# The first products of two expert layers, 36 and 136 columns wide in place of 256

## The reference

```python
# first expert layer: 8 experts, rank 16, the two best are taken
logits = x @ W_router.T                       # 8 columns
probs  = softmax(logits); combine = normalised weights of the two best
h      = einsum('nd,erd->ner', x, A)          # 8 * 16 = 128 columns
out    = x @ W_base.T + b_base + einsum('ner,eor->no', h * combine[:, :, None], B) * 2.0

# second expert layer: 4 experts, rank 8, the best one is taken
logits = x @ gate_w.T + expert_bias           # 4 columns
z      = einsum('nh,erh->ner', x, lora_A)     # 4 * 8 = 32 columns
out    = x @ W_up.T + (z of the best expert) @ lora_B
```

## Time and profile before

| | |
|---|---|
| median of 3 timed runs | 1790.31 us (1788.58 to 1790.43) |
| the profiled execution's own time | 1790.04 us |
| its span, first to last instruction | 1788.5 us |
| mean granted clock of TensorE | 0.974 |
| TensorE busy | 1688.1 us, 94% of the span |
| first expert layer, T(0) to the transposes of L697 | 154.8 to 189.3 us |
| second expert layer, block of the low parts to the end | 1723.5 to 1788.5 us |

### The profile page before, as it was taken

One profiled execution on the slowest core, in us unless ns is written; L12 is line 12 of the kernel. 1 busy time (PEld: TensorE's weight loads), 2 busy tenths in 40 slices (PEclk: granted clock), 3 DMA queues, 4 the chain that ended last, 5 costly groups with the idle time before them and its releaser, 6 DMA issues. The chain is left out here.

```text
span 1788.5 us, 26687 instructions
## 1 busy us (share of the span) xinstructions
PE 1688.1 (94%) x9420; PEld 1378.5 (77%) x9420; DVE 1199.0 (67%) x1847; ACT 1267.6 (71%) x2165; POOL 726.3 (41%) x786
## 2 busy tenths in 40 slices
PE   5998797999999999999999999999999999999839
PEld 4776575888888888888888888888888888888627
DVE  5565676766776677667766776677667766776853
ACT  3332146987798779877987798779877987798611
POOL 2543121444344434443444344434543454344620
PEclk9998898999999999999999999999999999999969
DMA  4220124333233323322333233323332323231121
GB/s 153 98 86 1 53 83 136 109 100 105 77 113 100 102 79 114 99 100 82 114 95 102 83 114 92 106 83 112 91 109 83 110 89 113 83 108 66 60 74 48
DMA packets 99429, 166.46 MB, mean 93 GB/s; under 512 B 11713, under 2 KB 49985, under 8 KB 97889
## 3 DMA queue, kind: packets, MB, share of 16 engines
q1 hardware_dynamic: 99296, 164.75, 28.8%
HBM read 158.43 MB, written 6.29 MB: 92 GB/s over the span
## 5 line engine op out<-in xcount | busy, mean ns | idle before, releaser
L217 PE MATMUL bank<-xh,w_h 128*128 128x512 f32 x1152 | 463.5, 402 | 9.6 <-DVE m_xc L1275 7.7
L218 PE MATMUL bank<-xl,w_h 128*128 128x512 f32 x1152 | 451.0, 392 | 0.0
L219 PE MATMUL bank<-xh,w_l 128*128 128x512 f32 x1152 | 450.1, 391 | 0.0
L1071 POOL TENSOR_TENSOR m_z_l<-m_zg,m_z_h 128x512 fp32r<-128x512 f32 x128 | 178.0, 1391 | 575.6 <-ACT m_z_h L1197 575.6
L1125 ACT ACTIVATE m_mt<-m_mt,m_unit 128x128 f32<-128x128 f32 x1024 | 312.1, 390 | 0.0
L1050 POOL TENSOR_TENSOR w_l<-w_raw,w_h 128x512 fp32r<-128x512 f32 x144 | 185.9, 1291 | 242.2 <-ACT w_h L1092 242.2
L1286 DVE TENSOR_TENSOR x<-x,bank 128x512 f32<-128x512 f32 x128 | 87.9, 687 | 273.7 <-PE bank L219 273.7
L217 PEld LDWEIGHTS bank<-xh,w_h 128*128 128x128 f32 x1152 | 217.4, 189 | 62.9 <-issue 19.7
L219 PEld LDWEIGHTS bank<-xh,w_l 128*128 128x128 f32 x1152 | 217.2, 189 | 46.5
L1275 DVE SCALAR_TENSOR_TENSOR m_xc<-bank,m_par_conv,m_xc 128x1020 f32<-128x1020 f32 (+2 forms) x192 | 244.6, 1274 | 12.0 <-ACT m_xc L1104 7.1
L218 PEld LDWEIGHTS bank<-xl,w_h 128*128 128x128 f32 x1152 | 217.6, 189 | 41.1
(11 more groups left out here) (238 smaller groups left out, 2771.6 us busy)
## 6 DMA issues: line engine op xcount, KB each, us to landing
m_mt<-ncs_rows SPq DMA_DIRECT2D x128, 512.0 KB, 3.8
w_raw<-w_in SPq DMA_DIRECT2D x144, 256.0 KB, 3.0
m_wo_raw<-w_out_in SPq DMA_DIRECT2D x64, 256.0 KB, 5.2
m_e<-ecs_rows SPq DMA_DIRECT2D x128, 128.0 KB, 3.5
a_wo_raw<-wo_in SPq DMA_DIRECT2D x8, 1024.0 KB, 4.9
x<-x_in SPq DMA_DIRECT2D x8, 256.0 KB, 4.6
a_wq_raw<-wq_in SPq DMA_DIRECT2D x8, 256.0 KB, 3.9
e_wb_raw<-f_base SPq DMA_DIRECT2D x2, 1024.0 KB, 7.8
```

Of the source, the lines that this page charges most:

```text
L217: nc.tensor.matmul(out, ah, bh, start=first, stop=False)
L218: nc.tensor.matmul(out, ah, bl, start=False, stop=False)
L219: return nc.tensor.matmul(out, al, bh, start=False, stop=last)
L1071: nc.gpsimd.tensor_tensor(z_l[:, s % 2, :, :], zg[:], f(z_h[:, s % 2, :, :]), ALU.subtract).then_inc(zl_ready, 1)
```

## The change

`a` becomes as wide as it needs to be: 136 columns in the first layer (544 numbers a row) and 36 in the second (144). The tile, its high and low part and the moving side of the 12 matmuls of each P(t) shrink with it. The zero fill, its semaphore and SyncE's wait for it are gone; with them goes `combine_block`'s whole program on GpSimd. Nothing is reordered.

```diff
-AW = 256
@@ attention_block, GpSimd @@
-                next_weights.pad(pool)
@@ ExpertWeights @@
-        self.a = [sb("wa_raw", [P, KT, AW]), sb("wa_h", [P, KT, AW], F32R), sb("wa_l", [P, KT, AW], F32R)]
+        width = self.ER + experts
+        self.a = [sb("wa_raw", [P, KT, width]), sb("wa_h", [P, KT, width], F32R), sb("wa_l", [P, KT, width], F32R)]
-        self.pad_zeroed = taken(nc, sems, f"{tag}_pad_zeroed")
-    def pad(self, pool):
-        self.nc.gpsimd.memset(self.a[0][:], 0.0).then_inc(self.pad_zeroed, 1)
-
     def load(self, sp):
...
-        sp.wait_ge(self.pad_zeroed, 1)
         sp.dma_start(raw[:, :, 0:ER], w_a).then_inc(self.loaded, 16)
@@ experts_block, products(t) @@
-                        last = three_pass(nc, bank[:, 2 + t % 2, 0:AW], xh[:, k, tok], xl[:, k, tok],
+                        last = three_pass(nc, bank[:, 2 + t % 2, 0:ER + experts], xh[:, k, tok], xl[:, k, tok],
                                           wa_h[:, k, :], wa_l[:, k, :], k == 0, k == KT - 1)
@@ combine_block @@
-            @block.gpsimd
-            def _(pool):
-                next_weights.pad(pool)
```

## The result

| | before | after |
|---|---|---|
| median of 10 timed runs each, side by side | 1790.45 us (1788.58 to 1792.23) | 1794.88 us (1793.9 to 1796.74) |
| profiled execution | 1790.04 us | 1794.77 us |
| its span | 1788.5 us | 1793.1 us |
| mean granted clock | 0.974 | 0.971 |
| first expert layer, T(0) to L697 (now L690) | 34.42 us | 35.07 us |

The ratio is 1.0027 (95% interval 1.0019 to 1.0036). The forecast was slower, 1796.4 us. The rows of the table from T(0) to the end of the second layer explain the profiled difference: T(0) starts at nearly the same time (1732.94 and 1732.87), and +0.74, +4.03, +1.52 and -1.56 follow, 4.7 us together.

What follows compares the result with a forecast made beforehand. GpSimd was taken to bound the second layer's entry, TensorE the rest. Entry -2.6, loads -0.7, clock +9.2 and first layer +0.2 made +6.1 on 1790.04 us, 1796.1; the timed median lies 0.3 above: 1796.4 us, range 1787.0 to 1801.0.

Steps and rivals of the forecast that it cites:

- zero fill and its wait: Two GpSimd fills of 0.95 us and SyncE's wait go; costed at 0, covered by the x loads.
- ScalarE's high part of A: Second layer's entry: 144 columns per row instead of 1024, 0.35 us instead of 1.06, -0.7 us.
- entry together, block to T(0): Second layer, block's start to first transposes: high part -0.7 and GpSimd's low part -1.9, together -2.6 us.
- a P product at full clock: Narrow products, both layers: the weight load bounds, 0.106 us each against 0.117 before.
- clock rises later, second layer: Second layer's start: thin first products delay steady streaming by 2.6 us, half of it lost, +1.3 us.
- T(3) to B(2): Second layer's narrow stretch: clock falls 4.5 us in, the rest takes twice as long, +5.9; narrower products -0.6 us.
- B(2) at half clock: Second layer: tile 2's wide base products start at half clock, half of 4.0 us lost, +2.0 us.
- first layer: Cheaper narrow products of tiles 1 to 4 -0.5, later clock rise +0.7, no fall of the clock: +0.2 us.
- the loads: Second layer: 72 narrow products at full clock, each now costing only its weight load, -0.7 us.
- The full-precision rate: Rival: narrow products run at the rate of full-precision matmuls, 0.23 us for 136 columns; 1795.4 to 1803 us, chance 0.11.
- the faster rival: Rival: narrow products shrink to their columns and VectorE decides, or clock holds and loads bound; 1782.4 to 1786.5 us, chance 0.10.
- That the clock holds: Rival: second layer's clock stays up or falls late in the narrow stretch; 1789.5 us, chance 0.22.

Runs made afterwards that it cites:

- e1_only: Kernel before with only the second layer's first products narrow (36 columns), zero fill and wait kept: 1795.48 us beside 1789.8, ratio 1.0028.
- e1_wide: Changed kernel, second layer's parts made on 36 columns but products 256 wide over zero fill: 1788.93 us beside 1789.8, ratio 0.9997.
- e1_136: Changed kernel, second layer's parts made on 36 columns but products 136 wide over zero fill: 1787.73 us beside 1789.44, ratio 0.9990.
- e0_only: Kernel before with only the first layer's first products narrow (136 columns): 1789.56 us beside 1789.8, ratio 1.0001.
- spread: Changed kernel, second layer's wide base products of tile 2 cut in four slices, one behind each of P(2) to P(5): 1787.2 us beside 1789.8, ratio 0.9991.
- dve_wide: Kernel before, with VectorE instead of GpSimd making the second layer's base low part: 1786.26 us beside 1789.44, ratio 0.9983.
- spread_wide: Kernel before, products 256 wide, second layer's base products of tile 2 in four slices behind P(2) to P(5): 1790.92 us beside 1789.44, ratio 1.0007.
- spread_dve: Changed kernel, second layer's base products of tile 2 spread among narrow products, and base low part on VectorE: 1785.21 us beside 1789.44, ratio 0.9976.
- w136_dve: Changed kernel, second layer's parts on 36 columns, products 136 wide over zeros, base low part on VectorE: 1783.84 us beside 1789.93, ratio 0.9970.

## Why the prediction held

The forecast's sign and its cause, a fall of the clock in the second layer that B(2) inherits, are shown: 36 columns lose it, 136 and 256 keep it with the rest of the kernel alike, and wide products between narrow ones keep it in the profile and, by their mean clock, in nine of eleven executions. By its own steps, in us of the profiled executions:

| step | predicted | measured | by |
|---|---|---|---|
| zero fill and its wait | 0 | not to be seen | weights requested 3.69 and 3.68 us behind x; `e1_only` keeps both and is as slow |
| ScalarE's high part of A | -0.7 | -0.74 for itself | 1.06 to 0.32 |
| entry together, block to T(0) | -2.6 with the high part | -1.13, without it | 9.48 to 8.35 |
| a P product at full clock | 0.106 | 0.11 | starts in both layers |
| clock rises later, second layer | +1.3 | T(0) to T(3) +0.74 | 13.27 to 14.01 |
| T(3) to B(2) | +5.9 - 0.6 | +4.03 | 10.98 to 15.01 |
| B(2) at half clock | +2.0 | +1.52 | 5.60 to 7.12 |
| first layer | +0.2 | T(0) to L697 +0.65 | 34.42 to 35.07 |
| last part | 0 | -1.56 | 25.69 to 24.13 |

**The total was in part luck.** The sum had +6.1 us; the profiles show +4.7 and the medians +4.4. It had +8.5 from T(0) to L697 of the second layer (9.2 for the clock, less 0.7 for the loads), where 6.3 were measured, and nothing for the last part, which gave 1.6 back. Against this, it had T(0) 2.4 us earlier, and it came 0.07 earlier. Two errors of over 2 us took each other away.

**The entry was mis-sized.** GpSimd's three parts did end 1.85 us sooner after the block's start, as predicted. That L142 would still meet them was wrong: L164, reached during the part of `b`, is held through both remaining parts, and 0.72 of the gain goes to the steps behind it. The prediction had this case among its bounds ("if L166 were itself held until the last part, 0.5 us would be given back (-1.4)"); the measured -1.1 lies 0.3 beyond that bound. In the profile the entry's whole gain then vanished in the later landing of the weights (T(0) only 0.07 us earlier). The lower ratios of `e1_wide` and `e1_136` agree with a gain that is there when the clock holds; their intervals reach 1.0006 and 0.9999, so each by itself shows little, and `e1_136` was also spared the second fall of the clock (below), which is worth as much.

**The moment of the fall was right, its price too high.** Predicted 4.5 us behind T(3), measured 4.6 (5.3 in `e1_only`). The 4.5 had been set above both rows it came from (2.5 and 3.8), so that it was met this closely is luck too. And the first of these rows was read wrongly: the 3.8 us behind the last wide matmul were not idle to their end, as TensorE's 0.63 us (x3) in 45.60 to 46.60 show; wide matmuls had started again at 45.97 when the clock fell. The second row stands as read. The work left would take 5.85 us at full clock (10.41 of `e1_136` less 4.56) and took 10.45, 1.8 times as long and not twice: +4.6 where the sum had +5.9. A tile's transposes and products took 3.33 us at half clock and 1.75 at full, 1.9 times; and at full clock (`e1_136`) P(7) waits 0.28 us for VectorE's low part, which half clock hides. A narrow product at half clock has its next one 0.21 behind it, as 256 columns do: the prediction's price for P(0) was right.

**The later rise is no fixed price.** T(0) to T(2) of the first layer took 10.22 us in the changed kernel and 10.24 in `e0_only`, against 9.17 before; but five other kernels with the same 136 columns there took 9.04 to 9.34. So what the forecast counted as +0.7 is 0 or 1.1, and its mean effect can't be told from these single profiles. In the second layer +1.3 was nearer than the +0.74 of the table says: T(0) to T(3) took 14.66 us in `e1_only`, 14.40 in `spread` and 14.58 in `e1_136`. The rise came 5.5 to 6.6 us behind T(0) in four kernels with 256 columns (8.3 in `dve_wide`) and 8.3 to 9.7 in the six with 36 or 136. So 136 columns keep the clock once it is up and still went with a late rise here. From T(2) to T(6) the first layer gained 0.42 in every kernel with 136 columns (10.24 to 9.82), near the 0.5 that the loads were to give. The median of `e0_only` bounds the whole layer between -1.4 and +1.6 us.

**The last part was not in the sum.** It gave back 1.56 us, since a second fall of the clock that stood there before was missing in this execution. It goes with the width in all profiles but one. The kernels with 256 columns in the second layer all had such a fall (before 1766.76, `e0_only` 1766.15, `e1_wide` 1763.51, `spread_wide` 1765.91, `dve_wide` 1762.93); of those with 36 or 136, `e1_only` had one (1769.88), and the changed kernel, `spread`, `e1_136`, `spread_dve` and `w136_dve` none. So part of what the mended kernels gain over the kernel before may stand here and not in the stretch of narrow products. What sets it was not tried.

**The rivals.** The full-precision rate is refuted by the spacing, also in the first layer:

```profile
164.96 0.28 PE L216 MATMUL bank<-e_wa_l,xh 128*128 128x136 f32 x1
165.07 0.27 PE L217 MATMUL bank<-e_wa_h,xl 128*128 128x136 f32 x1
165.18 0.28 PE L215 MATMUL bank<-e_wa_h,xh 128*128 128x136 f32 x1
```

0.11 us between starts, and the same for 36 columns, so columns do not count at these widths and what is left, the weight load, bounds. (In that rival's sum, 0.1 us on all 192 products would be 19 us and not the 8 that lead from 1795.4 to 1803; nothing hung on it.) That also refutes the faster rival. The Trainium skill, "TensorE: Matmul & The Clock Gate", section "Back-to-back issue gap", gives a formula on columns alone, by which 136 columns would take an estimated 59 ns; the measured 0.11 us goes against that reading and with its remark that a stream of load and matmul pairs is set by both. That the clock holds is refuted for 36 columns and true for 136. Whether the transposes in the stretch helped or not stays open: every kernel had them.

## What to carry to other kernels

Zero columns in the moving side can be worth keeping: where the weight load bounded, narrowing the matmul saved 0.01 us each, and a run of some 10 us of 36 wide ones cost about 5 us in clock, which 136 columns did not. Give each engine its own width: make the split parts only as wide as the data, fill the rest with zeros off the path, and run the products over enough of it. If a stretch of thin products can't be widened, put wide ones between them, and look at more than one execution, since here two of eleven still ran at the lower mean clock; and where VectorE's tiny steps set the path, look at what GpSimd still has in its list.

## What the hardware showed that was not expected

TensorE was busy 5.00 of 5.00 us, and its loads too, while the granted clock went to 0.50; the busy share does not tell whether the clock will hold. The 36 wide products did it 4.6 and 5.3 us behind T(3) in two kernels, the 136 wide ones at the same spacing in neither of two (`e1_136`, `w136_dve`). 100 of these 136 columns are zeros, and they served as well as the first layer's real ones, at which the clock stayed up in all seven kernels that have them.

A VectorE step on 8 numbers a row was held for 5.53 us through two instructions of GpSimd, one that was running when it came and one that came after it. The Trainium skill, "SBUF — State Buffer", section "SBUF: two separate sides", calls the pair of ports that the two engines share an exclusive lock that the one who starts first has for its whole instruction; of VectorE's instructions it names those in a two-port mode and those with two inputs from SBUF. The rows agree that the kind counts: in the kernel before, the reciprocal L141 took 0.20 us at 1726.10 while the part of `b` ran, and L142, with two inputs, was held from 1726.34 on. Which mode L164 ran in no run shows. The holds in these rows end with GpSimd's instructions, as by that rule, but the step did not get its turn between two of them. With one instruction fewer in the list the hold was 1.18 us.
